# Attention on one core: the same matmuls in another order, with the values and sums in twelve runs in place of thirteen

## The reference, cut to what matters

```python
scores = jnp.einsum('bhqd,bhkd->bhqk', q, k) / np.sqrt(HEAD_DIM).astype(np.float32)
attn = jax.nn.softmax(scores, axis=-1)
out = jnp.einsum('bhqk,bhkd->bhqd', attn, v)
...
src = x + _gqa(x, qw, qb, kw, kb, vw, vb, ow, ob)
src = _rmsnorm(src, norm1_w)
src = src + _moe(src, gate_w, w1, w2)
```

## Time and profile before

| | |
|---|---|
| median of 3 runs | 3295.18 us (3291.09 to 3295.74) |
| the profiled execution | 3294.3 us, span 3292.6 us |
| attention stage | about 1870 us of the span |
| TensorE busy in the span | 95% |
| VectorE, ScalarE, GpSimd | 64%, 49%, 61% |
| granted TensorE clock, mean | 0.964 |

### The profile page before, as it was taken

The page is one execution under the profiler, slowest core; times in us unless marked ns, Lnnn a source line. Parts: engine busy times, 40 slices in busy tenths (PEclk is TensorE's granted clock), DMA queues, the critical chain, the costliest instruction groups (busy, mean ns, idle before and its releaser), DMA issues. The chain is left out here.

```text
span 3292.6 us, 45482 instructions
## 1 busy us (share of the span) xinstructions
PE 3114.3 (95%) x16824; PEld 2008.3 (61%) x16824; DVE 2107.6 (64%) x3805; ACT 1608.7 (49%) x3249; POOL 2024.0 (61%) x880
## 2 busy tenths in 40 slices
PE   6998999999999999999999999984999999999992
PEld 5775444544544544544545445423999899889992
DVE  6888888788788788787787887813233333333334
ACT  3441566656556566565565665652333334334332
POOL 2442799889999999899899999882111111111114
PEclk8997899999999999999999999996999999999996
DMA  4564522011011022201101001022333333333237
GB/s 141 201 218 139 173 92 99 11 29 44 21 33 44 19 59 57 48 17 44 32 21 48 23 23 45 14 74 77 76 93 71 87 84 69 95 74 93 49 78 267
DMA packets 135519, 245.49 MB, mean 75 GB/s; under 512 B 30263, under 2 KB 35383, under 8 KB 132773
## 3 DMA queue, kind: packets, MB, share of 16 engines
q1 hardware_dynamic: 117232, 206.56, 19.6%
q0 software_dynamic: 16640, 35.42, 6.1%
q10 hardware_dynamic: 1461, 1.11, 0.1%
HBM read 127.82 MB, written 117.57 MB: 75 GB/s over the span
## 5 line engine op out<-in xcount | busy, mean ns | idle before, releaser
L1256 DVE TENSOR_REDUCE home_mxp<-p_ps_a 128x1 f32<-128x512 f32 x2021 | 1260.2, 679 | 282.7 <-PE p_ps_a L1455 274.0
L1175 ACT ACTIVATE p_PR<-p_ps_b 128x512 f32<-128x512 f32 x2048 | 1063.5, 604 | 705.4 <-PE p_ps_b L1469 695.2
L1036 POOL TENSOR_TENSOR p_PP<-p_PP,p_PR 128x2048 f32<-128x2048 f32 x223 | 1022.5, 4585 | 45.8 <-ACT p_PR L1175 23.1
L1455 PE MATMUL p_ps_a<-home_K,home_Q 96*128 96x512 f32 x2021 | 826.3, 436 | 19.8 <-DVE p_oh L1340 8.3
L1469 PE MATMUL p_ps_b<-home_Q,home_K 98*128 98x512 f32 x2048 | 784.0, 416 | 3.9 <-ACT p_PR L1175 3.7
L1032 POOL TENSOR_TENSOR p_PP<-p_PR 128x2048 f32<-128x2048 f32 x127 | 582.4, 4586 | 111.6 <-ACT p_PR L1175 100.7
L1455 PEld LDWEIGHTS p_ps_a<-home_K,home_Q 96*128 96x128 f32 x2021 | 383.4, 192 | 414.3 <-DVE home_mxp L1256 260.9
L1745 POOL DMA_INDIRECT src_d<-p_YE,p_token x80 | 123.5, 1543 | 830.2 <-DVE p_YE L1871 766.6
L1469 PEld LDWEIGHTS p_ps_b<-home_Q,home_K 98*128 98x128 f32 x2048 | 387.7, 190 | 234.9 <-ACT p_PR L1175 177.7
L1479 PE MATMUL p_ps_pv<-p_PR,p_VS 128*32 128x512 f32 x4096 | 524.6, 613 | 0.0
L1790 ACT ACTIVATE p_hf<-p_ps_h 128x384 f32<-128x384 f32 (+1 forms) x256 | 112.3, 439 | 577.1 <-PE p_ps_h L85 571.1
(11 more groups left out here) (194 smaller groups left out, 3243.0 us busy)
## 6 DMA issues: line engine op xcount, KB each, us to landing
weights_w_raw<-in_L_ffn_w SPq DMA_DIRECT2D x16, 2048.0 KB, 8.8
xe_d<-p_SR SPq DMA_DIRECT2D x20, 1056.0 KB, 9.8
home_Q<-qh_d SPq DMA_DIRECT2D x64, 256.0 KB, 3.8
p_XE<-xe_d SPq DMA_DIRECT2D x16, 792.0 KB, 4.7
src_d<-p_SR SPq DMA_DIRECT2D x9, 1024.0 KB, 6.4
p_XE<-xe_d SPq DMA_DIRECT2D x16, 528.0 KB, 3.6
p_X<-in_x SPq DMA_DIRECT2D x8, 1024.0 KB, 7.8
x_d<-p_x SPq DMA_DIRECT2D x8, 1024.0 KB, 5.4
```

Of the source, the lines that this page charges most:

```text
L1036: nc.gpsimd.tensor_tensor(PP[:, buf, :, :], PP[:, buf, :, :], PR[:, tile_at(u, tile), :, :], ALU.add).then_inc(add_made, 1)
L1175: nc.scalar.activation(PR[:, tile_at(u, kt), j, :], ps_b[:, n % BK, :], ACT.Exp, scale=SCALE).then_inc(ex_made, 1)
L1256: nc.vector.reduce_max(mxp[:, a // (S // CH), a % (S // CH):a % (S // CH) + 1], ps_a[:, bank, :], AXX).then_inc(a_read, 1)
L1455: nc.tensor.matmul(ps_a[:, bank, :], QS[u % QK][0:96, j, t * P:(t + 1) * P], KS[u % KV][0:96, kb * CH:(kb + 1) * CH], start=True, stop=Tru ...
```

## The change

Only the sixteen strings of `BASE` differ. The counts of each letter are the same, and so are `EXTRA`, the tiles at which other engines do their fixed work, and the instructions of GpSimd and SyncE in number and order.

```diff
-    BASE = ["ABABBAB", "ABVVBABABA", "BAABBABAV", "VDABBABAABAVAA",
-            "BBAABBA", "BVABABAB", "BABABAB", "VVABABBAB",
-            "VBABBAB", "AABABVVABABAA", "BBABAVB", "AADABABBABA",
-            "BBAABVDVABA", "ADABABABAB", "ABBABMBAVVA", "ABABABBAD"]
+    BASE = ["ABBABABV", "BABABB", "AAVVVABABABBAA", "BBAADABAB",
+            "ABABBABAA", "BBABAVVABA", "BABBAB", "ABVBBABA",
+            "VBABABB", "AABAVVVBABAB", "ABABBADABA", "AVABABAABB",
+            "BBAABBA", "AVAABABBAB", "BBABABAMVDVDVA", "ABABBABADA"]
```

## The result

The changed kernel takes **3274.39 us**, the median of 4 runs (3272.66 to 3276.51). The kernel before, run beside it, takes 3294.61 us (4 runs, 3291.09 to 3295.74). The ratio is 0.994 with a 95% interval of 0.9928 to 0.9952: 20.2 us less. The profiled executions took 3276.5 and 3294.3 us; on their basis 17.8 us were saved, where 7.5 were forecast.

A forecast was written before the change was run, and what follows sets the result against it. The prediction took TensorE's queue in the attention stage as the bound: -12.0 us from the clock and +4.5 from the remaining terms gave -7.5, so 3286.8 profiled and 3288 us as median, with a range of 3280 to 3300.

The forecast's parts named there:

- clean: Nine intervals from M to M (g=2 to g=3, and the first chunk's three): 55.21 us forecast, +0.74 each.
- with O: Seven intervals from M to M holding two O's (g=3 to g=0): 59.81 us forecast, -0.11 each.
- with R: Seven intervals from M to M holding two O's and the R's (g=0 to g=1): 62.18 us forecast, +0.56 each.
- L, N, K: Seven intervals (g=1 to g=2): 57.85 us forecast, -0.93 against a walked 58.78, plus 1.7 a chunk from the clock.
- The price of a run: Each run of V and D costs TensorE some 0.34 us; one run less in each of 32 units, -11 us.
- The clock costs 1.7 us a chunk: TensorE's lowered clock behind the choice lengthens the interval with L, N, K; regaining it in seven chunks gives -12.0 us.
- the walk: The prediction's letter-by-letter timing of TensorE's queue in both orders, with assumed delays for reader starts and released banks.
- The stalls grow by 1.08, to 2.9: In a clean unit, TensorE's stalls on readers grow by 1.08 us to 2.9, against 0.34 saved by the run.
- the drains decide alone: Rival: stalls don't grow, the 1.08 per unit fall away, -34 us, 3254; half is 3271; chance 0.06 for both.
- The fall goes with the stall: Behind N, the third A's 1.18 us stall for the choice vanishes and the clock's fall with it: -12.0 us.
- the clock falls by N's small matmuls alone: Rival: the clock still falls once a chunk, by N's 0.9 us of tiny matmuls; 3300 or 3294 us, chance 0.2.
- The run of five starves nobody: VDVDV behind the M takes 4.4 us at full clock; the rival, that it starves readers or clock, had chance 0.07.

The follow-up runs named there:

- e3: The kernel after with one VVV in tile 9 split by a B, so thirteen runs in every unit; 3285.54 us, ratio 0.9968 to before.
- e1: The kernel before with, only in unit g=2, the run VVD three letters behind N in place of eight; 3279.89 us, ratio 0.9954 to before.
- e5: The kernel before with the choice's eight index lookups replaced by two constants, output not the reference's; 3284.82 us, ratio 0.997 to before.
- e4: The kernel after with A's and B's of tiles 11 and 12 in turn, so no four B's together; 3270.8 us, ratio 0.9923 to before.
- e2: The kernel after with, only in unit g=2, the run VVV six letters later, eight behind N; 3310.57 us, ratio 1.0042 to before.
- e6: The kernel after with tiles 11 and 12 in turn and three of GpSimd's g=3 sends behind its addition of tile 12; 3264.04 us, ratio 0.9904 to before.

## Why the prediction was wrong

The mechanisms were right and the direction too. What failed are sizes: two terms of the sum, the clock with the order around N (-2.64 us a chunk, measured -3.28) and the stalls of each unit (+1.08, measured some +0.9), and the slack that it gave GpSimd in the intervals with O. All erred to the same side. In us of the profiled execution:

| term | forecast | measured | miss x count |
|---|---|---|---|
| clean, 9 | +0.74 | +0.52 | -2.0 |
| with O, 7 | -0.11 | -0.34 | -1.6 |
| with R, 7 | +0.56 | +0.22 | -2.4 |
| L, N, K, 7 | -2.64 (-0.93 and -1.7) | -3.28 | -4.5 |
| outside | +1.2 (twice 0.6) | +1.4 | +0.2 |

The misses sum to -10.3 us, and -7.5 less 10.3 is -17.8, as measured. That the last row fits is luck, as this part of the span varies by 5 us between profiles.

- **The price of a run** (0.34 us, -11 us in all) was right: 0.29 to 0.33 in e3.
- **"The clock costs 1.7 us a chunk"**, worked out as the trace's 60.49 less a walked 58.78, failed in size, as did **-0.93** for the order. Both hung on that walked number. e1 gives a measured one: in before's order, with neither stall nor fall, the interval has a mean of 57.21. So 3.28 us of before's 60.49 were stall and fall together: the stall is 1.18, and the fall 2.1, if the moved run itself costs nothing. With the stall and at full clock the interval would take 58.39, and the walk was 0.39 too long. After has the same mean of 57.21, but partly by chance: in six chunks it is 0.08 above e1, in the last one 0.50 below, and why wasn't sought. For single chunks the fall costs 1.4 to 1.6 us where it is short (59.96 less the 57.26 of the same chunk in e1, less 1.18; 1.4 in e5) and 2.8 to 2.9 where it is long (61.30, less 57.29, less 1.18).
- **"The stalls grow by 1.08, to 2.9"** failed in size. With 0.34 saved by the run and a clean interval of +0.52, they grew by 0.86 (0.81 with the lowest price of e3), and counted by segment they are 2.6. The segment that the prediction called the worst was right: 0.78 against 0.74, and e4 puts 0.52 on its four B's, where the prediction had 0.50 for the sixth. So was the one of 18 letters (0.29 against 0.31). The one ahead of the M was too high (0.66 against 0.80). "The segments of before lose at most 0.3 each" was off: the one of tiles 11 and 12 lost 0.38. Which choice in the walk (0.43 us for the readers' start, 0.06 for a released bank) makes it too high wasn't tested, and the miss of the intervals with R, 0.34 us each, has no cause found. The rival by which the drains decide alone did not hold either: stalls grew, by four fifths of what was walked.
- **GpSimd "has slack"** was read off the clean intervals. In those with O it had none, in before already: there the D of tile 15 stood for it in five of seven, 0.18 to 0.30 us.

```profile
1265.34 1.07 PE L1493 MATMUL p_ps_den<-p_PP,p_ones 128*32 128x512 f32 x8 [0.30 <-POOL p_PP L1036]
```

  In after none stands: the D comes 7.4 us after the M in place of 5.6. In the two intervals of before without this wait (59.78 and 59.75), the change is -0.13 and -0.04, next to the forecast -0.11; the rest of the -0.34 is the wait that went away. "The walk has it ready in time" was right for after, and by little: in e1's order TensorE waits 1.23 us for the addition, in e4, where a unit is another 0.5 us shorter, 0.74.
- **The fall goes with the stall**: with the stall taken away the fall was gone, seven of seven, in after and in e1, and with the stall back (e2) it was back, seven of seven. Its rival, that the clock falls by N's small matmuls alone, is excluded: N is in after and e1 unchanged. But a stall doesn't always bring a fall, as e5's fifth chunk shows, and that short waits elsewhere bring none, as the prediction said, holds for the 30 intervals and not for the end of the stage, as the last section shows. The Trainium skill, page "TensorE: Matmul & The Clock Gate", section "A second HAM failure mode: psum-queue depth-cycling", tells of frequent short idling between groups of matmuls that makes the clock go up and down. Here one such idling a chunk was enough behind N, with 0.66, 1.18 and 1.87 us.
- **The run of five starves nobody**: right. 4.43 us, clock at 1.00, no interval below.
- **The range** was the other mistake: it ended at 3280, "a saving of half as much again", though the walk's own free numbers moved all 30 units the same way. An error of 0.2 us in a unit is 6 us. Three kinds of interval met within 0.1 us in the old order say little on stalls that the old order hardly had (1.8 us walked, against 2.9).

## What to carry to other kernels

Compare such a kernel from mark to mark, by kind of interval: a change of 0.6% was seven intervals out of thirty, while shares of busy time and sums of waits didn't show it. Where a queue must wait for another engine's chain behind tiny matmuls, put long work that needs neither the held bank nor that engine ahead of the waiting instruction: here three V's took away 1.18 us of stall and some 2 us of lowered clock a chunk. When a model has been fitted on an order with few stalls, give its forecast of many stalls a range in units of the repeated step, and when the bound engine gets shorter, look at the next one's slack in each interval, not in the stage.

## What the runs showed of the hardware

- Behind N, the clock's fall does not scale with the stall. 0.66 us of idling gave a fall of 3.4 us in six of seven chunks and none in one; 1.18 us gave 3.4 us in four and 6.8 us in three; 1.87 us gave 6.8 us in all seven. A wait of 1.23 us elsewhere brought none: e1's D ahead of 1262.01, with the clock at 1.00 (1260.40 to 1263.80). Behind N there are also 0.9 us of eight-column matmuls ahead of the wait; whether they are the difference was not tested.
- Neither small matmuls nor one long wait are needed for a fall. At the end of the stage, where no A's are left, TensorE goes at the pace of the exponentials, a B every 0.49 us, with listed waits of 0.31 us at most up to 2181.2 us of after. There the clock fell:

```profile
2178.78 2.46 PE L1469 MATMUL p_ps_b<-home_Q,home_K 98*128 98x512 f32 x5 [0.31 <-ACT p_PR L1175]
...
2181.20:2184.40 3.20, 3.20 (x17) 0.77 (x20) 0.00 (x0) 0.96 (x2) 3.20 (x1) 0.50 0.14 49
```

  Five such B's at 2130.82 in after were followed by a clock of 1.00, and five in the same place of e6 by a fall (0.50 from 2123.80 to 2127.20). In before, a wait of 2.10 us for GpSimd in this part was followed by one too:

```profile
2196.49 1.94 PE L1493 MATMUL p_ps_den<-p_PP,p_ones 128*32 128x512 f32 x8 [2.10 <-POOL p_PP L1036]
...
2196.50:2199.90 3.40, 3.40 (x16) 0.59 (x16) 0.00 (x0) 0.00 (x0) 3.29 (x2) 0.51 0.11 41
```

- Four-way column tiles keep the clock up: 4.43 us of nothing but V and D, 31 times in after, at 1.00.
- Entering and leaving such a run costs 0.29 to 0.33 us in every kind of interval. An L directly behind a run of V saves that too: in after a V and the L behind it take 1.85 us together (1151.76 to 1153.61), as two V's do.
